# One-hots of both halves of a step made in one instruction of 128x4096

## The reference

```
x = layernorm(x + attn(x))        # decay, update, gate; scan over the sequence; W_out
x = layernorm(x + ffn(x))

# ffn: h = 8 heads, nk = 32 keys a side, ne = 1024 experts, k = 8
xn  = batchnorm(x) * gamma + beta
sim = einsum(xn @ w_q.T, keys)                 # two sides, 32 scores each
sx, ix = top_k(sim[0], 8); sy, iy = top_k(sim[1], 8)
scores, pk = top_k(all sums sx + sy, 8); idx = ix * 32 + iy at pk
o = gelu(x . key_in[idx]) * softmax(scores)
y = sum over heads and k of o * key_out[idx]
```

## Time and profile before

| what | value |
|---|---|
| median of 3 runs | 595.89 us (594.94 to 597.73) |
| the profiled execution | 595.74 us, of which span 593.9 us, and 1.84 us around it |
| granted TensorE clock, mean | 0.716 |
| VectorE busy | 515.8 us, 87% |
| TensorE busy | 315.1 us, 53% |
| GpSimd busy | 287.0 us, 48% |
| ScalarE busy | 257.7 us, 43% |

### The profile page before, as it was taken

How to read it: one execution, slowest core, us unless ns; L and a number is a source line. 1 busy time by engine, 2 the same in 40 slices (tenths; PEclk the granted TensorE clock), 3 DMA queues, 4 the chain that set the end, 5 groups by cost and what they waited for, 6 DMA issues and landing times. The chain is left out here.

```text
span 593.9 us, 15355 instructions
## 1 busy us (share of the span) xinstructions
PE 315.1 (53%) x5105; PEld 204.8 (34%) x5105; DVE 515.8 (87%) x3289; ACT 257.7 (43%) x400; POOL 287.0 (48%) x307
## 2 busy tenths in 40 slices
PE   6687585124232827282836284637453655275854
PEld 3233462013122325232722272226222522262454
DVE  2557796999999999999979997999799999994944
ACT  4776523322242543373355325632663257125721
POOL 1143421252536479367826782688268736960000
PEclk9897865665665767685868575858585959587988
DMA  8700000000014002300410050005000500050061
GB/s 241 223 0 2 0 1 1 1 1 3 2 34 112 1 3 68 78 19 1 114 51 1 0 134 27 1 1 141 19 1 1 142 18 1 4 142 1 2 165 31
DMA packets 49839, 26.50 MB, mean 45 GB/s; under 512 B 3056, under 2 KB 49008, under 8 KB 49776
## 3 DMA queue, kind: packets, MB, share of 16 engines
q1 hardware_dynamic: 49200, 25.70, 16.5%
q10 hardware_dynamic: 576, 0.07, 0.1%
HBM read 6.88 MB, written 2.10 MB: 15 GB/s over the span
## 5 line engine op out<-in xcount | busy, mean ns | idle before, releaser
L935 PE MATMUL psum<-arena 64*64 64x64 f16 x4096 | 55.4, 222 | 121.6 <-DVE arena L690 108.0
L935 PEld LDWEIGHTS psum<-arena 64*64 64x64 f16 x4096 | 51.6, 135 | 135.2 <-issue 110.3
L707 DVE FIND_INDEX8 idx<-vals,sims 128x8 uint32<-128x32 f32 x512 | 82.7, 185 | 0.0
L959 PE MATMUL psum<-ko,arena 128*128 128x128 f32 x512 | 67.9, 300 | 21.2 <-POOL arena L335 13.4
L959 PEld LDWEIGHTS psum<-ko,arena 128*128 128x128 f32 x512 | 66.4, 215 | 30.0 <-POOL arena L335 21.2
L335 POOL TENSOR_TENSOR arena<-arena 128x512 f32<-128x512 f32 x48 | 71.8, 1528 | 0.0
L949 PE MATMUL psum<-x1T,trn 128*128 128x512 f32 (+1 forms) x128 | 63.9, 645 | 12.7 <-ACT arena L483 12.7
L301 POOL COPY words<-words 128x320 uint16<-128x320 uint16 x16 | 38.1, 2381 | 55.6 <-DVE words L729 55.6
L476 ACT ACTIVATE arena<-psum 128x1024 f32<-128x1024 f32 x32 | 32.6, 1018 | 74.1 <-DMA arena<-stage 47.7
L700 DVE MAX8 vals<-sims 128x8 f32<-128x32 f32 x512 | 49.1, 176 | 12.3 <-issue 8.8
L913 PE MATMUL psum<-msim,xn 128*128 128x512 f32 x64 | 56.0, 1027 | 4.6 <-ACT xn L440 4.6
(11 more groups left out here) (110 smaller groups left out, 703.8 us busy)
## 6 DMA issues: line engine op xcount, KB each, us to landing
arena<-arena SPq DMA_DIRECT2D x64, 128.0 KB
arena<-stage SPq DMA_DIRECT2D x64, 128.0 KB
stage<-in_L_attn_x_dram SPq DMA_DIRECT2D x8, 256.0 KB, 4.2
x<-in_L_attn_x_dram SPq DMA_DIRECT2D x4, 512.0 KB, 7.0
out_dram<-nat SPq DMA_DIRECT2D x8, 256.0 KB, 2.2
nat<-in_L_ffn_key_in_dram SPq DMA_DIRECT2D x4, 128.0 KB, 3.6
ko<-in_L_ffn_key_out_dram SPq DMA_DIRECT2D x4, 128.0 KB, 3.7
nat<-in_L_ffn_keys_dram SPq DMA_DIRECT2D x2, 128.0 KB, 2.7
```

The lines of the kernel that those rows point to most:

```text
L707: last = dve.max_index(idx[:, p, t * H + h, :], vals[:, p, t * H + h, :], sims[:, t, r, :])
L935: last = pe.matmul(psum[64 * e:64 * e + 64, at:at + 2 * NK], hotx[rows, par, two, :, e].rearrange("p b i -> p (b i)"), hotw[rows, par, par ...
L959: last = pe.matmul(to[:, t * P:(t + 1) * P], a[:, jh, t * P:(t + 1) * P], ko[:, jh, :], start=(jh == 0), stop=(jh == JH - 1))
```

## The change

The halves are no longer made one after the other. Each of the four kinds is one instruction of 128x4096, so four instructions a step. `hot_y` stands where the first half's y and x stood, `hot_x` behind the candidates' MAX8, `hot_high` behind the marks and `hot_low` behind the marked codes. `hot_done` and `hoty_done` count steps, not halves; both scatter halves wait for the same `hot_done`. `hot_x` waits for both scatters of two steps before. The one-hots of step 15, behind the last step, are four instructions in a row.

```diff
             def lists_out(m):
                 wait(act, "lists_mm", m + 1)
-                wait(act, "hot_done", m * 2)
+                wait(act, "hot_done", m)
...
-            def hot_slice(hf):
-                return slice(32 * hf, 32 * hf + 32)
-
-            def spread(f, hf):
-                v = listsT[:, f, 64 * hf:64 * hf + 64].rearrange("p (g s) -> p g s", s=2)
-                return v.unsqueeze(2).to_broadcast([P, 32, NK, 2])
-
-
-            def hot_y(m, hf):
+            def spread(f):
+                v = listsT[:, f, :].rearrange("p (g s) -> p g s", s=2)
+                return v.unsqueeze(2).to_broadcast([P, 64, NK, 2])
+
+
+            def hot_y(m):
                 wait(dve, "lists_evac", m + 1)
-                dve.tensor_tensor(hoty[:, hot_slice(hf)], iota[:, 1].unsqueeze(1).to_broadcast([P, 32, NK, 2]),
-                                  spread(1, hf), ALU.is_equal).then_inc(s["hoty_done"], 1)
-
-            def hot_x(m, par, hf):
-                wait(dve, "p_mm", m * 2 - 3 + hf)
-                dve.tensor_tensor(hotx[:, par, hot_slice(hf)], iota[:, 0].unsqueeze(1).to_broadcast([P, 32, NK, 2]),
-                                  spread(0, hf), ALU.is_equal)
-
-            def hot_w(m, par, hf):
-                wait(dve, "hoty_done", m * 2 + (hf + 1))
-                dve.tensor_tensor(hotw[:, par, 0, hot_slice(hf)], hoty[:, hot_slice(hf)], spread(2, hf),
-                                  ALU.mult)
-                dve.tensor_tensor(hotw[:, par, 1, hot_slice(hf)], hoty[:, hot_slice(hf)], spread(3, hf),
-                                  ALU.mult).then_inc(s["hot_done"], 1)
+                dve.tensor_tensor(hoty[:, :], iota[:, 1].unsqueeze(1).to_broadcast([P, 64, NK, 2]),
+                                  spread(1), ALU.is_equal).then_inc(s["hoty_done"], 1)
+
+            def hot_x(m, par):
+                wait(dve, "p_mm", m * 2 - 2)
+                dve.tensor_tensor(hotx[:, par], iota[:, 0].unsqueeze(1).to_broadcast([P, 64, NK, 2]),
+                                  spread(0), ALU.is_equal)
+
+            def hot_high(m, par):
+                wait(dve, "hoty_done", m + 1)
+                dve.tensor_tensor(hotw[:, par, 0], hoty[:, :], spread(2), ALU.mult)
+
+            def hot_low(m, par):
+                dve.tensor_tensor(hotw[:, par, 1], hoty[:, :], spread(3), ALU.mult).then_inc(s["hot_done"], 1)
...
                 if hot_before:
-                    hot_y(m - 1, 0)
-                    hot_x(m - 1, hot_par, 0)
+                    hot_y(m - 1)
                 hold(dve, "cand_done", m + 1)
...
                 if hot_before:
-                    hot_w(m - 1, hot_par, 0)
-                    hot_y(m - 1, 1)
+                    hot_x(m - 1, hot_par)
...
                 if hot_before:
-                    hot_x(m - 1, hot_par, 1)
+                    hot_high(m - 1, hot_par)
...
                 if hot_before:
-                    hot_w(m - 1, hot_par, 1)
+                    hot_low(m - 1, hot_par)
...
-            for hf in range(2):
-                hot_y(T // 2 - 1, hf)
-                hot_x(T // 2 - 1, 1, hf)
-                hot_w(T // 2 - 1, 1, hf)
+            hot_y(T // 2 - 1)
+            hot_x(T // 2 - 1, 1)
+            hot_high(T // 2 - 1, 1)
+            hot_low(T // 2 - 1, 1)
...
                 wait(pe, "p_evac", m * 4 + 2 * hf)
-                hold(pe, "hot_done", m * 2 + (hf + 1))
+                hold(pe, "hot_done", m + 1)
```

## The result

The changed kernel takes 600.09 us (median of 4 runs, 599.83 to 601.70), the kernel before 595.65 in the same comparison (4 runs). The ratio is 1.0083, 95% interval 1.0048 to 1.0117: slower by 4.4 us or 0.8%. The forecast was 597.5 us, range 593.1 to 601.0. The profiled execution of the changed kernel is the slowest of its four, 601.70 us with a span of 599.9.

What follows compares the result with a forecast made beforehand. The prediction took VectorE, busy 87% of the span, as the bound until step 15, then a chain of engines and transfers. 595.74 - 3.8 + 3.4 + 0.7 + 2.7 - 1.3 = 597.4, so 597.5 us; range 593.1 to 601.0.

Steps and rivals of the forecast that it cites:

- (a): VectorE, steps 1 to 15: 60 fewer one-hot instructions at 0.063 us each, -3.8 us (-3.7 to -5.8).
- The rival of 0.19 an instruction: VectorE's one-hots: a dearer fixed part per instruction, saving 11.4 us in all, total 589.9 us; chance 7%.
- (b): Odd steps, quads 2 to 6: VectorE's scales wait 0.69 us for ScalarE's square root, five times, +3.4 us.
- (c): sims_out in even steps: VectorE waits 0.73 us for late scores once, +0.7 us (0 to 0.8); later even steps free.
- (d): Tail: halves no longer overlap, first scatter 4.3 us later, TensorE's clock lower after idling; +2.7 us (1.5 to 3.5).
- (e): Before step 15's lists: scatter and experts fill TensorE's idle gap, so its clock stays up; -1.3 us (0 to -1.4).
- (f): Things with one answer: GpSimd's code sum, stricter waits of hot_x and hot_done, and a transfer's release; no cost.
- Full clock in the scatters: TensorE's scatters stay at full clock, so square root waits and tail cost less; 593.1 us, chance 10%.
- TensorE at the lower clock through the tail: Tail: no gain before step 15's lists, second scatter and last expert matmuls slower; 601.7 us, chance 18%.
- the merge does nothing: One-hots: 4096 elements take more than twice 2048, or the same instructions come out; 601.3 us, chance 5%.

Runs made afterwards that it cites:

- f2: The changed kernel with each one-hot kind again as two instructions of 128x2048 in a row, order and announcements kept; 601.30 us, ratio 1.0101 to the kernel before.
- e4: The changed kernel with ScalarE's square root moved ahead of the evacuation p_out(q, 0, 0); 596.88 us, ratio 1.0053 to the kernel before.
- e1: The changed kernel run again without any edit, for a second profile; 599.95 us, ratio 1.0131 to the kernel before.
- e3: The changed kernel with only the one-hots behind the last step made and announced in two halves; 597.58 us, ratio 1.0065 to the kernel before.

## Why the prediction was right, and where not

**(a) The instructions: right.** -3.8 was forecast, 0.25 us a step. Steps without any wait last 27.94 us where they lasted 28.19 (step 4), 27.95 for 28.20 (step 6), 27.93 for 28.19 (step 14). With f2 the figure is up to 0.08 an instruction rather than 0.063. The rival of 0.19 an instruction is out: it would have shown 0.76 a step.

**(b) The square root: right.** +3.4 forecast, 3.2 measured (0.71 and four times 0.62), 3.7 given back by e4. The chain summed from rows was 6.97; in quad 4 it ended within 0.1 of it.

**(c) The scores of step 3: right.** 0.7 forecast, 0.65 to 0.66 in all eight profiles with late announcement. No even step from 4 on waited for scores, as forecast; ScalarE sat idle only 0.75 us ahead of `convert` there, where the earlier trace rows had 7.99, so the cover is nearly used up.

**(d) The tail: right without the pauses.** +2.7 forecast. C is 50.9 in e1 for 48.0 to 48.9 before, +2.1 to +3.0, and e3 gives 2.8 back. The working rounds up a little: 576.8 less 575.38 is 1.4, not 1.5. The lower clock after 4.7 us of idleness came as I took it from the earlier trace rows (1.93 for the scatter, and 0.50 granted). In executions with pauses another 3 to 4 us come on top, and they are in no row of before.

**(e) What the tail gets back: the step that failed for the profile it was made against.** -1.3 was forecast against the first profile of before. B fell by 0.7 there and by 0.3 in e1, and 0.25 of either is the cheaper one-hots of step 15, which (a) had counted. TensorE was idle only 1.97 and 2.95 us, as expected, but that did not fix its clock: 1.00 in one execution and 0.50 in the other at 540 us. And where the clock was up, a pause of 0.80 took the gain. Against the median of five profiles of before B did fall, by 1.2 (e1) and 1.6. I had taken one execution's 3.44 and 1.30 for the usual case; in the four others the same records took 3.57 to 3.78 and 1.29 to 1.93, and B was 0.8 to 1.2 longer in three of them.

**(f) The rest: right, with a term missing.** GpSimd's codes and the stricter waits cost nothing. But the list of "things with one answer" did not ask what fewer instructions do to the place of the loop: three gaps of 0.8 to 1.0 us, 2.6 us in all. That is the size of the distance between 597.5 and 600.1. The list also left out the 0.7 us by which the instructions that make the codes are slower. The earlier trace rows had shown the kind of cost (8.8 us of issue behind the branch), and I read it as fixed.

**The rivals.** Full clock in the scatters: out, in steps 0 to 13 every scatter of both profiles took 1.93 or 1.94. TensorE at the lower clock through the tail, 601.7: its time is near the one measured, but not its mechanism; the second scatter ran at full clock in both profiles, which was its point of decision. That the merge does nothing: out, 2.20 us from one start to the next for 4096 elements, where two of 2048 take 2.26.

The measured 600.1 is just over the bound of 598.9, in the direction to which I had given 0.27. The sum with the missing term (597.5 + 2.6) gives it, but in part by luck. Over A, B and C, all that the change touches, the changed kernel took 6.2 us (e1) and 9.3 us (with pauses) more than the profile before, where 1.7 was forecast. Against the usual execution before (493.4 us over the three, the median of five) it is 4.2 and 7.2. The head was 3.3 and 3.5 us shorter than in the profile before, which no part of the change explains, and that brought the total back into the range. The range's own ends are not sums either: the upper ends of the terms add up to 599.8, not 600.3, and no sum stands behind 601.0.

## What to carry to other kernels

Merging two instructions saves their fixed part, 0.06 to 0.08 us here, but it also merges their announcements: look at what the first half's early announcement had hidden, and put what other engines need soonest (here a square root of 0.3 us behind 1.95 us of evacuations) ahead in their queues. Where only the last batch is exposed, keep it in halves and merge the rest. And after any edit that changes the number of instructions ahead of a loop, compare the first instructions behind its branch and the count of instruction transfers with those before.

## What the runs showed of the hardware

A loop of VectorE, 421 to 433 instructions long, paid 2.8 to 3.1 us behind each branch in every profile. It paid another 0.8 to 1.1 us (13 instructions ahead of a block's end) or 1.6 to 1.8 us (5 ahead) each time round, and none of this with 11 behind it. The second block arrived 2.1 to 2.4 us after the loop's first instruction had started. VectorE's blocks came as packets of 8192 bytes, TensorE's as packets of 16384, and the engine went on 1.1 to 1.4 us after the end of the packet that it waited for. TensorE's pauses, in four of thirteen executions, were 0.4 to 2.3 us, 254 instructions apart. And a matmul group in the same place of the same kernel took 1.99 or 3.40 us, with the granted clock at 1.00 or 0.50, after idle times of 1.97 and 2.95 us.
